# Last mixture of a four-layer gated network: whole normalised rows scattered by the routing, expert tiles read as plain blocks

## The reference, cut to what matters

```python
TOP_K = 8; CAPACITY = 128                      # 64 experts, width 96
x = hidden_states.reshape(-1, H)               # normalised rows, (2048, 256)
probs = softmax(x @ router_weight.T)           # (2048, 64)
topw, topi = top_k(probs, K); topw = topw / sum(topw)
pos = cumsum(one_hot(topi.reshape(-1)))[...] - 1   # place of each choice within its expert
xe = zeros((E, C, H)).at[flat_e, pos].set(repeat(x, K), mode='drop')
g, u = split(xe @ gate_up_proj); ye = (silu(g) * u) @ down_proj
y = sum over the 8 choices of topw * ye[flat_e, pos], 0 where pos >= C
x = x + tanh(g_ffn[3]) * y
```

## Time and profile before

| | |
|---|---|
| median of 3 runs | 2811.33 us (2806.39 to 2815.75) |
| the profiled execution | 2816.71 us, span 2815.0 us |
| busy share of the span | PE 80%, PEld 54%, DVE 47%, ACT 42%, POOL 41% |
| mean granted TensorE clock | 0.892 of full speed |
| DMA | 205.71 MB, mean 73 GB/s |

### The profile page before, as it was taken

The page is one execution under the profiler, slowest core; times in us unless marked ns, Lnnn a source line. Parts: engine busy times, 40 slices in busy tenths (PEclk is TensorE's granted clock), DMA queues, the critical chain, the costliest instruction groups (busy, mean ns, idle before and its releaser), DMA issues.

```text
span 2815.0 us, 37152 instructions
## 1 busy us (share of the span) xinstructions
PE 2259.1 (80%) x11057; PEld 1511.2 (54%) x11057; DVE 1330.9 (47%) x3439; ACT 1172.6 (42%) x3936; POOL 1150.8 (41%) x1118
## 2 busy tenths in 40 slices
PE   5999999689999779599999978999588576614653
PEld 4666667566776456366666644566344333204552
DVE  2433443476676533365555524333556674721112
ACT  3444443355555443356655533333266263401111
POOL 0211111233444345344454532255434546546665
PEclk8999999899999889799999989999788677856777
DMA  9991002000000226300000024466702000004676
GB/s 348 357 350 61 1 1 61 1 1 1 17 7 11 78 63 100 99 1 1 1 23 11 33 71 121 93 102 104 169 5 72 1 8 8 1 8 104 133 155 140
DMA packets 198669, 205.71 MB, mean 73 GB/s; under 512 B 29033, under 2 KB 189305, under 8 KB 197706
## 3 DMA queue, kind: packets, MB, share of 16 engines
q1 hardware_dynamic: 159050, 152.81, 18.1%
q0 software_dynamic: 39424, 50.53, 10.2%
HBM read 91.12 MB, written 112.20 MB: 72 GB/s over the span
## 4 chain that ended last, share of the span: by engine, by line
PE 45%; issue 26%; DVE 12%; DMA 5%; ACT 5%; POOL 4%; SPq 1%; another core or an unknown queue 1%; POOLq 0%; DVEq 0%; ACTq 0%
PE ps L133 38%; ACT work L959 2%; DMA moe_sum<-work,weights 2%; POOL slots L2839 2%; PE ps L1119 1%; DMA work<-xn_rows,weights 1%; DVE xn L249 1%; PE ps L2086 1%; PE ps L2101 1%; PE ps L556 1%; POOL work L2916 1%; PE ps L223 1%; DVE n_mx L1213 1%; DVE bn L235 1%
## 5 line engine op out<-in xcount | busy, mean ns | idle before, releaser
L133 PE MATMUL ps<-work,weights 128*128 128x512 f32 (+4 forms) x1712 | 652.8, 522 | 22.9 <-issue 12.8
L133 PE MATMUL ps<-weights,work 128*128 128x126 f32 (+6 forms) x2816 | 638.3, 358 | 15.1 <-DVE weights L436 10.1
L133 PEld LDWEIGHTS ps<-weights,work 128*128 128x128 f32 (+2 forms) x2816 | 412.6, 196 | 65.0 <-DVE weights L436 12.2
L133 PE MATMUL ps<-xn_T,weights 128*128 128x512 f32 (+5 forms) x1040 | 381.7, 502 | 19.5 <-DVE weights L1369 6.7
L133 PEld LDWEIGHTS ps<-work,weights 128*128 128x128 f32 (+3 forms) x1712 | 278.1, 203 | 154.6 <-issue 106.7
L2164 POOL DMA_INDIRECT f_sum<-work x120 | 185.3, 1544 | 190.9 <-ACT work L2125 162.8
L726 POOL TENSOR_TENSOR work<-work,rinv 128x512 f32<-128x512 f32 x128 | 133.3, 1041 | 304.5 <-DVE rinv L676 281.3
L133 PEld LDWEIGHTS ps<-xn_T,weights 128*128 128x128 f32 (+3 forms) x1040 | 165.9, 191 | 122.9 <-issue 104.3
L1238 POOL TENSOR_TENSOR work<-weights,head_sel 128x512 f32<-128x512 f32 x128 | 134.2, 1053 | 230.3 <-PE ps L133 203.3
L1188 ACT ACTIVATE work<-ps,n_negm 128x128 f32<-128x128 f32 x512 | 145.2, 370 | 135.9 <-DVE n_negm L1215 132.4
L959 ACT ACTIVATE work<-ps,n_negm 128x112 f32<-128x112 f32 (+1 forms) x512 | 152.2, 347 | 78.7 <-DVE n_negm L987 78.5
(11 more groups left out here) (298 smaller groups left out, 3829.3 us busy)
## 6 DMA issues: line engine op xcount, KB each, us to landing
f_rows<-weights SPq DMA_DIRECT2D x25, 2176.0 KB, 19.5
work<-f_rows SPq DMA_DIRECT2D x120, 136.0 KB, 2.5
weights<-in_L_ffn_gate_up_proj SPq DMA_DIRECT2D x16, 768.0 KB
f_sum<-weights SPq DMA_DIRECT2D x4, 2176.0 KB, 16.4
weights<-in_L_ffn_W SPq DMA_DIRECT2D x96, 88.0 KB
weights<-in_L_ffn_down_proj SPq DMA_DIRECT2D x16, 384.0 KB
moe_sum<-weights POOLq DMA_DIRECT2D x2, 2176.0 KB
weights<-in_L_xattn_Wo SPq DMA_DIRECT2D x2, 2048.0 KB, 11.2
```

The lines of the kernel that those rows point to most:

```text
L133: return nc.tensor.matmul(out, lhsT, rhs, start=start, stop=stop, skip_group_check=True)
```

## The change

The routing scatters whole rows of ROW3 = 324 columns (1296 bytes): 256 columns of the normalised row, the token number, and 64 weights (zero where the expert wasn't chosen). The normalisation writes into one of two row tiles `f3_rows` (by the body's parity) in place of XN. An expert's tile is rows e, 64 + e, 128 + e and so on of the DRAM table, which SP loads with one plain DMA; the token numbers of the addition and the weight of each row come out of that tile. The gathers, the table of pairs and its read, the stores of `xn_rows` and the one-hots are gone. The mask comes from `match_replace` and a comparison, the slots from a maximum over the masked map. The filling of the new row table (4 blocks of 16 x 128 rows) and of the two accumulators moves to the program's start. POOL's wait for the body before's scatters is gone; DVE waits for the scatters of two bodies before, ahead of the normalisation and ahead of the cast of the slots.

```diff
     def rows_init(sp, rows, sums):
...
+        for b in range(0, n, ROW_BLOCKS):
+            m = min(ROW_BLOCKS, n - b)
+            sp.dma_start(rows[:, b:b + m, :], row_blank[:, 0:row].unsqueeze(1).broadcast_to([P, m, row])).then_inc(rows_zeroed, 16)
...
-                tail_dve_norm(dve, S.n, S.prev, (xs_stored, s) if A.split else None)
+                tail_dve_norm(dve, S.n, S.prev, (rows_written[S.prev % 2], S.prev // 2) if S.prev >= 2 else None, f3_rows[S.prev % 2])
...
-    def l3_store(sp, n, s, prev):
-        done(sp, xn_ready, n, 0)
-        sp.dma_start(xs_rows[:, bass.ds(prev * TB, TB), :], XN[:, :, 0:D]).then_inc(xs_stored.sem, 16)
...
     def f3_sp(sp):
-        l3_store(sp, NS * 7 + NS - 1, 0, NS - 1)
-        sp.wait_ge(tab_written.sem, tab_written.end)
-        sp.dma_start(f3_tab[:, 0:L3E, :], table_rows).then_inc(tab_read, 16)
-        for g in range(1, NG):
-            for q in range(GE // QE):
-                done(sp, f3_y_mm, 0, (g - 1) * GE + (q + 1) * QE - 1)
-                f3_weights(sp, g, q)
+        for sig in rows_written:
+            sp.wait_ge(sig.sem, sig.end)
+        for e in range(L3E):
+            if e >= XR:
+                done(sp, f3_added[e % 2], 0, 16 * ((e - XR) // 2) + 15)
+            sp.dma_start(f3_xe[:, e % XR, :], xrows_of[:, e, :]).then_inc(f3_rows_in[e % XR].sem, 16)
+            last = e - XR + 2
+            if last >= 0 and last % QE == QE - 1 and last // QE + GE // QE < L3E // QE:
+                done(sp, f3_y_mm, 0, last)
+                f3_weights(sp, last // GE + 1, last % GE // QE)
...
     def f3_route_pool(pool, s, start=0, end=TB * L3K):
         if start == 0:
             done(pool, f3_slots_ready, s, 0)
-            done(pool, tab_written, s, -1)
         for i in range(start, end):
             t, k = divmod(i, L3K)
-            nc.gpsimd.indirect_dma_start(table, bass.IndirectOffsetOnAxis(ap=f3_slot_u[:, t, k:k + 1], axis=0),
-                                         f3_pay[:, t, k, :], None, bounds_check=SLOTS - 1, oob_is_err=False)\
-                .then_inc(tab_written.sem, 16)
+            nc.gpsimd.indirect_dma_start(xrows, bass.IndirectOffsetOnAxis(ap=f3_slot_u[:, s % 2, t, k:k + 1], axis=0),
+                                         f3_rows[s % 2][:, t, :], None, bounds_check=SLOTS - 1, oob_is_err=False)\
+                .then_inc(rows_written[s % 2].sem, 16)
...
     def f3_choices(dve, r, link):
-        link(nc.vector.tensor_tensor(f3_oh.rearrange("p t k e -> p (t k) e"), iota[:, 0:L3E].unsqueeze(1).broadcast_to([P, TB * L3K, L3E]),
-                                     R3.ixf.rearrange("p t k -> p (t k)").unsqueeze(2).broadcast_to([P, TB * L3K, L3E]), ALU.is_equal))
-            nc.vector.tensor_reduce(f3_m, f3_oh.rearrange("p t k e -> p t e k"), AX.X, ALU.add).then_inc(f3_m_ready.sem, 1)
+        for t in range(TB):
+            ins = nc.vector.max(R.top[:, t, :], R.e[:, t, :])
+        link(ins)
+        for t in range(TB):
+            nc.vector.match_replace(f3_left[:, t, :], R.top[:, t, :], R.e[:, t, :], -1.0)
+        link(nc.vector.tensor_reduce(den, R.top, AX.X, ALU.add))
+            nc.vector.tensor_scalar(f3_m, f3_left, 0.0, None, ALU.is_lt).then_inc(f3_m_ready.sem, 1)
+        link(nc.vector.reciprocal(den, den))
+        link(nc.vector.scalar_tensor_tensor(R.c, f3_left, 0.0, R.e, ALU.is_lt, ALU.mult))
...
-        link(nc.vector.tensor_tensor(f3_oh, f3_oh, f3_map.unsqueeze(2).broadcast_to([P, TB, L3K, L3E]), ALU.mult))
-        link(nc.vector.tensor_reduce(f3_slot, f3_oh, AX.X, ALU.add))
-        link(nc.vector.tensor_copy(f3_slot_u, f3_slot))
+        link(nc.vector.tensor_tensor(f3_map, f3_map, f3_m, ALU.mult))
+        for t in range(TB):
+            ins = nc.vector.max(f3_slot[:, t, :], f3_map[:, t, :])
+        link(ins)
+        if r >= 2:
+            done(dve, rows_written[r % 2], r // 2, -1)
+        link(nc.vector.tensor_scalar(f3_slot_u[:, r % 2], f3_slot, -1.0, None, ALU.add))
...
     def f3_pool(pool):
-        pool.wait_ge(tab_read, 16)
-        pool.wait_ge(xs_stored.sem, 16 * (1 + NS))
-        for e in range(AHEAD):
-            f3_gather(pool, e)
         for e in range(L3E):
-            if e + AHEAD < L3E:
-                done(pool, f3_xt_tr, 0, e + AHEAD - XR)
-                f3_gather(pool, e + AHEAD)
             done(pool, f3_y_ready, 0, e)
             done(pool, f3_added[e % 2], 0, 16 * (e // 2) - 1)
```

More of the change, by code:

```diff
@@ L61, in semaphore @@
         return ctx.enter_context(nc.semaphore(name))
-    def dma_signal(name, first):
-        return Signal(semaphore(name), 16, NS, 16 * first)
     def signal(name, per, bodies=NS):
@@ L222, in tail_pe_xn @@
         for t in range(TB):
-            last = nc.tensor.transpose(TP[:, t * P:(t + 1) * P], XN[:, t, k * P:(k + 1) * P], ident[:])
+            last = nc.tensor.transpose(TP[:, t * P:(t + 1) * P], xn[:, t, k * P:(k + 1) * P], ident[:])
         last.then_inc(xn_tr.sem, 1)
@@ L1682, in _build @@
     ROW_BLOCKS = 16
-    row_inits = 16 * sum(2 + -(-F.rows // (ROW_BLOCKS * P)) for F in (F1, F2))
+    L3E, L3F, L3K = 64, 96, 8
+    SLOTS = P * L3E
+    xrows = nc.dram_tensor("f3_rows", (SLOTS, ROW3), F32, kind="Internal").ap()
+    acc = [nc.dram_tensor(f"moe_sum{i}", ((B + 1) * P, D), F32, kind="Internal").ap() for i in range(2)]
+    xrows_of = xrows.rearrange("(p e) c -> p e c", e=L3E)
+    tables_of_rows = [(F.dram.rearrange("(b p) c -> p b c", p=P), F.acc) for F in (F1, F2)] + [(xrows_of, acc)]
+    row_inits = 16 * sum(2 + -(-rows.shape[1] // ROW_BLOCKS) for rows, _ in tables_of_rows)
     def rows_blank(ordered):
@@ L3018, in _ @@
         sp.dma_start(l1_bias[:], a["L1_xattn_bout"].rearrange("(k p) -> p k", p=P)).then_inc(in_l1x, 16)
-        rows_init(sp, F1)
-        rows_init(sp, F2)
+        for rows, sums in tables_of_rows:
+            rows_init(sp, rows, sums)
         sp.wait_ge(L0.y_mm.sem, L0.y_mm.value(NS - 1, HEADS - 1))
@@ L3049, in _ @@
         sums_sp(sp, F2)
-        sp.wait_ge(pool_consts, 5)
-        sp.dma_start(xs[B * P:, :], l3_zero_row).then_inc(xs_stored.sem, 16)
         f3_loads(sp)
-        for s in range(1, NS):
-            n, prev = tail_of(L3.stage, s)
-            l3_store(sp, n, s, prev)
         f3_sp(sp)
```

113 lines of the change are left out of this document (42 added, 71 removed).

## The result

| | before | change |
|---|---|---|
| median of 4 runs | 2808.86 us (2806.12 to 2815.75) | 2761.64 us (2756.20 to 2765.23) |
| ratio | | 0.9823, 95% interval 0.9808 to 0.9838 |
| profiled execution, span | 2816.71, 2815.0 us | 2761.39, 2759.7 us |

The change is faster by 47 us between the medians and by 55 us between the two profiled executions. It lies in the range (2716 to 2788); 2750 was forecast.

The account below looks back on a forecast made before the run. DVE's route then POOL's scatters were taken to pace the routes, POOL the expert loop. Gains 31.2 + 2.3 + 28.2 = 61.7 us from 2816.7 give 2755.0, less 5.4 for the median: 2750 us, range 2716 to 2788.

Parts of the forecast that it names:

- three routes beside attention: Routing in three bodies beside attention: shorter DVE passes save 7.8 us each, taken as all on the path.
- expert loop: First to last addition: 198 us for 226.2, gain 28 us, at 2.4 us per expert plus 3.9 per pair of weight loads.
- Routing on DVE: Each of four routes: 10.42 us of passes removed, 2.6 added, net 7.8 us; 31.2 us in all.
- Scatters: POOL's 32 scatters per body: no change expected with rows of 1296 bytes for 8.
- rival D: Whole-row scatters slow POOL by up to 1.16 us each, 148 us against 62 gained: 2898 us; chance 0.08.
- Last body to first expert: From SP's table read to the first transpose: one plain tile load replaces two round trips, 2.3 us gone.
- SP's list: Tile and weight loads share SP's list; tiles asked for 8 experts ahead, some 19 us: nothing expected.
- rival C: The 16 DMA engines, not POOL, set the expert loop: it stays at 224 us, gain 36 us, 2776; chance 0.18.
- The start: Extra fills and zeroes at program start: 44 us more on SP, covered by 190 us before its next load.
- From the trace to the median: Whole kernel: 5.4 us taken off 2755.0 because before's profiled execution was that much slower than its median.
- Rival B: Transitions between bodies: late matmuls vanish with the 8-byte pairs, 2 x 8 us more gained, 2734 us; chance 0.12.
- rival E: The change doesn't reach the path and the loop is as in C: a few us, 2803 to 2811; chance 0.04.

Follow-up runs that it names:

- first pair: The first traces of before and of the change: profiled executions of 2816.71 and 2761.39 us.
- the pair on one chip: Before and the change run once more without edit, in the third set: 2780.75 us for before, 2730.13 us for the change, ratio 0.9826.
- the passes put back: The changed kernel with the four old DVE passes of 2048 columns added as unused work: 2770.78 us, ratio to before 0.9964.
- the choice alone: The kernel before with only the new way of choosing (match_replace, comparison, maximum for slots); pairs, table and gathers stay: 2776.97 us, ratio to before 0.9871.
- the third chip: Chip of the third set of runs, where before and the change ran once more: before 2780.75 us, change 2730.13 us.
- all four edits: The change with weights loaded one expert at a time, four accumulators (eight result buffers), last tail's deviation earlier on POOL, 24 scatters spread: 2662.80 us, ratio to before 0.9578.
- the first set: First of three sets of experiments, each on one chip with its own runs of before; its median of before was 2812.7 us.
- the first experiment: The kernel before with only the new way of choosing, in place of the four 2048-column passes: 2776.97 us, ratio to before 0.9871.
- four accumulators: The changed kernel with four DRAM accumulators for two and eight result buffers for four: 2741.70 us, ratio to before 0.9749.
- weights by one: The changed kernel with the same weights loaded one expert at a time instead of four: 2732.68 us, ratio to before 0.9700.

## Why the prediction was right, and where it was off

The sum was made for the profiled execution: 61.7 us. Its terms, against the first pair of traces and against the pair on one chip:

| term | forecast | first pair | one chip |
|---|---|---|---|
| three routes beside attention | 23.4 | 4.8 + 7.3 + 7.4 = 19.5 | 8.5 + 7.1 + 6.5 = 22.0 |
| last route | 7.8 | 9.5 | 9.6 |
| 32 last scatters | 0 | 2.5 | 2.6 |
| last scatter to first transpose | 2.3 | 2.5 | 2.6 |
| first transpose to first addition | 0 | -0.5 | -0.6 |
| expert loop | 28.2 | 21.5 | 18.4 |
| last addition to end | 0 | 0.2 | -0.2 |
| sum | 61.7 | 55.3 | 54.4 |

**Routing on DVE: right.** The added instructions came as priced: 0.42 per pass of 256 columns (the comparison into bf16 only 0.29), 0.61 for four MAX where 0.88 was taken, and MATCH_REPLACE as long as the index search:

```profile
L2867 DVE MATCH_REPLACE8 weights<-weights 128x64 f32<-128x64 f32 x16 | 3.2, 209 | 0.0
```

That all four routes are on the path was taken from POOL's wait and the chain; the passes put back show it, at 10.1, 9.7 and 10.6 us in three routes and some 8 in the first. What they and the choice alone show together: of some 50 us, 36 to 41 hang on DVE's passes. The last route gave 9.5 and not 7.8. On DVE, from the first MAX to the slots, the last route is 9.9 us shorter: the added instructions took some 0.5 less than priced, the small casts, products and copies removed were 0.5 more, and 0.8 is a wait of DVE for PE's count of positions, which the sum had not seen. It stands in the trace of before:

```profile
2499.32 0.42 DVE L2894 SCALAR_TENSOR_TENSOR weights<-ps,iota 128x256 f32<-128x256 f32 x1 [0.84 <-PE ps L133]
```

In the change DVE's new passes over the weights fill that time. That the first route gave 4.8 in one pair and 8.5 in the other is no effect of the change: the change's trace of the first pair runs 2.1 us late by 72 us already, and by 4.1 us when the fourth attention begins (2024.69 for 2020.60). Counted from there, the first route gave 8.9 us, and 7.6 in the pair on one chip, where the change was 0.9 ahead.

**Scatters: right, with a gain not foreseen.** The pitch stayed 1.28 us with 1296-byte rows and 8-byte pairs alike (0.97 busy), so rival D had no point to decide from. The growth by bytes of the Trainium skill's fit ("DMA: Bandwidth & Descriptors", the SWDGE path in the anatomy of one DMA), 0.38 us per scatter by the estimate in the prediction, is not seen: POOL doesn't wait for the flight, and from POOL's last scatter to SP's next DMA, which waits for its landing, 2.13 us pass with pairs (2548.56 to 2550.69) and 2.17 with rows (2517.02 to 2519.19). The 2.5 us gained are one gap in all three traces with pairs (before twice, and the new choice alone), which the change doesn't have:

```profile
2497.59 0.97 POOL L2839 DMA_INDIRECT slots<-weights  x1 [2.92 <-issue]
```

What stands in it was not tried.

**Last body to first expert: right**, 2.5 to 2.6 for 2.3. Last scatter to first transpose is now 4.46 us (2517.02 to 2521.48).

**The expert loop: the wait is the one named, one term was too small.** In the free stretch 2.37 us per expert came for 2.4. The stall at each of the 12 loads was put at 3.9 and is 4.7 in the period shown, near the upper bound of 4.9: 63 x 2.37 + 12 x 4.65 = 205.1 for 204.7 measured, 7 us over the forecast of 198.

The step that failed is the one on SP's list. "Tiles are asked for 8 experts ahead, some 19 us" is not so: SP asks for tile e once the addition of e - 8 has *landed*, and by then PE has transposed all tiles before e but one, at most two (e = 8 to 63 in the change's first trace). The prediction set PE less than two experts from the additions; in the trace it is four or five ahead of the last one issued, and only a landed one gives its room back, so little is left of the ring of eight. From request to transpose 2.2 to 6.4 us pass, and 5.3 to 9.5 behind a load of weights, for the 19 assumed. A late landing so delays the next tile as well, that tile is late itself behind the same burst (9.47 us), and PE stands for 2 to 5 us where I had written "nothing expected". (PE's whole wait for tiles over the loop, 69 us on the third chip, is not all loss: in the loop of before it waited 83 us for gathers.)

So rival C was half true. The DMA engines alone did not set the loop (their share over it is 0.77 to 0.78, and 0.93 with all four edits), but they are full in the bursts, and these are what the 12 stalls come from: without the loads the loop is 154 us, with the same bytes in small pieces 184. The rival's sentence from the Trainium skill ("DMA: Bandwidth & Descriptors", issuing engines are not separate DMA queues), that all queues end in the same 16 engines, agrees with this: weights and tiles are issued by SP and additions by POOL, and tiles and additions both come late in a burst with a share of 0.97. Whether they wait in the engines or at DRAM no run tells.

The other half of that section of the Trainium skill, that moving an issue saves only issuing time, is not contradicted: POOL lost 64 us of busy time, and the loop 21.5. How much of that 21.5 is POOL's relief and how much the plain loads in place of gathers was not separated.

**The start: right.** Zeroes and fills took 13.4 and 29.0 us for 44 in all, they end at 258 us, and SP's next load comes at 455.27 us, for 453.13 before. The offset of 2.1 us between the first two traces exists before the fills of the new table begin and is unchanged at 322 us.

**From the trace to the median: a term that did not carry.** I took 5.4 us off because the profiled execution of before was slow by as much. That of the change stood at its own median (2761.39 for 2761.64), so against the other executions the gain was 47 and not 62. Of the miss of 11.6 us, 6.4 are in the sum (the loop 6.7 and the routes 2.2 short, the scatters' gap 2.5 over), and some 5 are this correction. The total so came nearer than its parts: the scatters' gap, which was not foreseen, made up for part of the loop, and that much is luck. One execution stands for a kernel no better than its spread, 10 us here.

**Rival B** (late matmuls vanish, 16 us) did not come, and for a reason that none of the theories had: they go with the set of runs, not with the kernel. The traces of the first pair and of the first set all have them in these transitions, with pairs and with rows; in the two later sets none has. Each set ran on a chip and at a time of its own, so chip and time are not told apart. In the change's first trace:

```profile
2226.06 0.89 DVE L2594 TENSOR_TENSOR weights<-ps,weights 128x128 f32<-128x128 f32 x4 [2.84 <-remote]
2238.69 0.88 DVE L2594 TENSOR_TENSOR weights<-ps,weights 128x128 f32<-128x128 f32 x4 [4.66 <-remote]
```

Without them the distance of two routes of the kernel before is 106 us and with them 114.5.

**Rival D** fell with the pitch of 1.28 us, and **rival E** fell with the first experiment.

## What to carry to other kernels

A pass over a one-hot of choices x experts costs by its columns; if the values are distinct, a maximum, a match_replace and a comparison say the same in columns of experts alone. On an engine that ends a wait in every body, nearly each microsecond of it comes back as often as there are bodies (8 to 10.6 us of 10.4 here). When the issuing engine of a loop is relieved, ask next what each queue does in a burst: cutting a 1.1 MB prefetch into pieces of one step, and giving the read-modify-writes more than two targets, was worth more than the relief itself (together 47 us of loop, less 15 at the end, for 18 to 21). How far ahead a load is asked for is counted from the event that releases its buffer, not from the size of the ring.

## What the runs showed that was not expected

- The same program differs by 1.1% between sets on different chips: 2812.7, 2785.7 and 2780.8 us for the kernel before. Some 17 of the 36 us between two traces of it lie in two transitions where matmuls end late by a releaser that the trace does not name (DVE waits of 1.2 to 8.1 us in before, up to 10.2 in the change). What causes them is open.
- Four passes of 10.4 us, on DVE alone, cost 9.7 to 10.1 us of span in a body of 99 us whose DVE is busy for less than two thirds of it.
- An addition of 128 rows of 1 KB lands 3.5 us after it is issued, and 8.6 us when 1.1 MB of weights is in flight.
- The granted clock in the expert loop was higher wherever the loop was shorter than the change's: 0.82 in the change (third set), 0.87 with four accumulators, 0.91 with weights by one, 0.93 with all four edits, 0.94 without loads. It doesn't follow the loop's length alone: with four accumulators the loop is 169.6 us, with weights by one 184.0. What part of the gains it carries was not tried.
